# A fused cross-attention and gated feed-forward kernel on one core: steps change their place in the order of issue

## The reference

```python
def rmsnorm(x, w):
    return x * rsqrt(mean(x * x) + 1e-6) * w

# cross-attention
text = layernorm(x)                       # over the width
f    = rmsnorm(ctx, fn_w)
Q    = rmsnorm(text @ Wq.T + Wq_b, qn_w)
K    = rmsnorm(f @ Wk.T + Wk_b, kn_w)
attn = softmax(Q @ K.T / sqrt(1024))
x    = x + tanh(g_xattn) * (attn @ f)

# feed-forward with 8 gated low-rank experts
z    = layernorm(x)
base = z @ W_base.T + b_base
gate = softmax(z @ W_gate.T)
thr  = sigmoid(z @ W_thr + b_thr) * 0.125
w    = relu(gate - thr); w = w / (sum(w), or 1 where that is 0)
h    = z @ A.T                            # 8 experts x 16
moe  = sum over experts (h * w) @ B * 2
x    = x + tanh(g_ffn) * (base + moe)
```

## Time and profile before

| what | value |
|---|---|
| time, median of 3 runs | 473.6 us (472.96 to 475.18) |
| profiled execution, its span | 473.6 us |
| PE busy | 468.0 us, 99% |
| DVE busy | 361.7 us, 76% |
| ACT busy | 173.8 us, 37% |
| POOL busy | 119.8 us, 25% |
| DMA | 84.40 MB, 178 GB/s in the mean |
| key-weight stage (`m`) on PE | 85.05 to 107.27 us |
| products with `gram` (`y`, `s`, `attend`) on PE | 107.27 to 239.6 us |
| last stage, pair 0 | 239.6 to 272.4 us |
| last stage, pairs 1 to 7 | 272.4 us to the end |

### The profile page before, as it was taken

The page is one execution under the profiler, slowest core; times in us unless marked ns, Lnnn a source line. Parts: engine busy times, 40 slices in busy tenths (PEclk is TensorE's granted clock), DMA queues, the critical chain, the costliest instruction groups (busy, mean ns, idle before and its releaser), DMA issues.

```text
span 473.6 us, 6945 instructions
## 1 busy us (share of the span) xinstructions
PE 468.0 (99%) x2481; PEld 399.3 (84%) x2481; DVE 361.7 (76%) x750; ACT 173.8 (37%) x349; POOL 119.8 (25%) x107
## 2 busy tenths in 40 slices
PE   8999999999999999999999999999999999999997
PEld 7898999998887888888888888878888888888886
DVE  1687996588888978879987888968777678877733
ACT  5847532332224305226334625342241421414300
POOL 0020511002344253345242406031230502205000
PEclk9999999999999999999999999999999999999999
DMA  8993129958576378576379640221405032050202
GB/s 320 412 408 118 76 90 389 405 183 286 197 246 248 133 252 283 193 292 229 141 273 419 277 144 36 81 98 46 133 1 175 4 89 90 2 177 1 89 1 89
DMA packets 22114, 84.40 MB, mean 178 GB/s; under 512 B 2624, under 2 KB 3904, under 8 KB 19264
## 3 DMA queue, kind: packets, MB, share of 16 engines
q1 hardware_dynamic: 21792, 83.81, 48.2%
q10 hardware_dynamic: 288, 0.15, 0.1%
HBM read 61.93 MB, written 22.02 MB: 177 GB/s over the span
## 4 chain that ended last, share of the span: by engine, by line
PE 78%; DVE 8%; DMA 8%; issue 3%; ACT 1%; POOL 1%; SPq 0%; DVEq 0%; ACTq 0%
PE bank L769 10%; PE bank L773 10%; PE bank L771 10%; PE bank L649 6%; PE bank L685 5%; PE bank L687 5%; PE bank L686 5%; PE bank L530 4%; PE bank L742 4%; DMA xst<-x_dram 3%; DMA T_low<-t_low_T 2%; DMA xz<-xt_dram 2%; DMA out_dram<-xs 2%; PE bank L599 2%; DVE wl_B L1438 1%
## 5 line engine op out<-in xcount | busy, mean ns | idle before, releaser
L1554 POOL TENSOR_TENSOR small<-small,tiny 128x1 f32<-128x1 f32 (+2 forms) x25 | 23.6, 942 | 167.1 <-DVE small L1183 137.9
L1534 DVE SCALAR_TENSOR_TENSOR xs<-bank,tiny,xs 128x512 f32<-128x512 f32 (+1 forms) x61 | 43.3, 739 | 20.6 <-PE bank L773 14.9
L685 PE MATMUL bank<-xth,gram 128*128 128x512 f32 x144 | 57.3, 398 | 0.0
L687 PE MATMUL bank<-xtl,gram 128*128 128x512 f32 x144 | 56.3, 391 | 0.0
L686 PE MATMUL bank<-xth,gram 128*128 128x512 f32 x144 | 56.1, 390 | 0.0
L769 PE MATMUL bank<-wh_B,zh 128*128 128x512 f32 x116 | 47.0, 405 | 0.1
L769 PE MATMUL bank<-wh_T,zh 128*128 128x512 f32 (+1 forms) x116 | 46.6, 402 | 0.0
L1582 POOL TENSOR_TENSOR sq_sum<-sq_sum,sq 128x512 f32<-128x512 f32 x24 | 32.0, 1333 | 56.5 <-DVE sq L1362 56.5
L773 PE MATMUL bank<-wh_B,zl 128*128 128x512 f32 x116 | 45.6, 393 | 0.0
L771 PE MATMUL bank<-wl_B,zh 128*128 128x512 f32 x116 | 45.4, 391 | 0.0
L773 PE MATMUL bank<-wh_T,zl 128*128 128x512 f32 (+1 forms) x116 | 44.7, 386 | 0.0
(11 more groups left out here) (200 smaller groups left out, 1133.2 us busy)
## 6 DMA issues: line engine op xcount, KB each, us to landing
xst<-x_dram SPq DMA_DIRECT2D x16, 512.0 KB, 4.4
xz<-xt_dram SPq DMA_DIRECT2D x16, 512.0 KB, 7.6
out_dram<-xs SPq DMA_DIRECT2D x14, 512.0 KB, 2.7
xa<-x_dram SPq DMA_DIRECT2D x12, 512.0 KB, 3.4
x<-xa SPq DMA_DIRECT2D x12, 512.0 KB, 3.0
xs<-x SPq DMA_DIRECT2D x12, 512.0 KB, 4.0
wq_raw<-wq_dram SPq DMA_DIRECT2D x8, 512.0 KB, 13.8
t_raw_T<-wb_dram SPq DMA_DIRECT2D x4, 1024.0 KB, 16.7
```

The lines of the kernel that those rows point to most:

```text
L685: pe.matmul(acc[:, :], gram[:, g, 0, :], xth[b % 2][:, r, :], start=r == ROWS[j][0], stop=False)
L687: done = pe.matmul(acc[:, :], gram[:, g, 0, :], xtl[b % 2][:, r, :], start=False, stop=r == ROWS[j][-1])
L1534: dve.scalar_tensor_tensor(out=xs[slot][:, cols], in0=bank[n_bank][:, 0:hi - lo], scalar=tg[:, 1:2], in1=xs[slot][:, cols], op0=ALU.mult, ...
```

## The change

Five groups of steps change their place in the list. No instruction is added or removed, and no tile or wait changes.

1. In the key-weight stage `x_stat 6` goes from behind `m_out 1` to behind `m_out 2`, `x_stat 7` and `z 0 0` from behind `m_out 2` to behind `m_out 3`, `z 0 1` from behind `m_out 3` to behind `m_out 4`.
2. In batches 1 to 3, after `y b 2`, `shares` and `fn_low` go ahead of the next batch's `z` and `zh` quarter 0.
3. `bias 1` goes from ahead of `y 3 7` to behind it.
4. In pair 0 `split B22 1` goes from behind `mt 0` to right behind `split B22 0`, ahead of `fn_norm 3` and `chosen 1`.
5. In pairs 1 to 6 `stat t1`, the statistics of the second tile, goes from behind the second product to behind the third, and so behind `mt` of the second tile and, in pair 1, behind `split T4 0`.

```diff
--- before.py
+++ after.py
@@ -377,8 +377,8 @@
         for r in range(KB):
             first += [("m", r), ("m_out", r)]
             first += [("zh", 0, r - 3)] * (3 <= r < 7)
-            first += {0: [("x_stat", 5), ("load_xt", 0)], 1: [("x_stat", 6)], 2: [("x_stat", 7), ("z", 0, 0)],
-                      3: [("z", 0, 1)], 4: [("z", 0, 2), ("zl", 0, 0)], 5: [("z", 0, 3), ("zl", 0, 1)],
+            first += {0: [("x_stat", 5), ("load_xt", 0)], 1: [], 2: [("x_stat", 6)], 3: [("x_stat", 7), ("z", 0, 0)],
+                      4: [("z", 0, 1), ("z", 0, 2), ("zl", 0, 0)], 5: [("z", 0, 3), ("zl", 0, 1)],
                       6: [("zl", 0, 2)], 7: [("zl", 0, 3)]}[r]
         first += [("load_xt", 1)]
         for b in range(B):
@@ -389,10 +389,12 @@
                               3: [("bb",), ("bias", 0)],
                               5: [("zt", 0, "a11"), ("stat", 1)],
                               6: [("zt", 0, "a12"), ("xn", 1), ("head_w",)],
-                              7: [("zt", 0, "a21"), ("bias", 1)]}.get(j, [])
+                              7: [("zt", 0, "a21")]}.get(j, [])
                 if j == 1 and b + 1 < B:
                     first.append(("mr", b + 1))
                 first.append(("y", b, j))
+                if (b, j) == (B - 1, 7):
+                    first.append(("bias", 1))
                 if (b, j) == (B - 1, 4):
                     first.append(("load_hd",))
                 if b == 0:
@@ -400,6 +402,8 @@
                     first += {4: [("load_fn", 0)], 6: [("load_xa", 0), ("load_xa", 1)], 7: [("load_bb",)]}.get(j, [])
                 if b == 1 and 1 < j < 4:
                     first.append(("x_stat", 12 + j))
+                if b > 0 and j == 2:
+                    first += [("shares", b - 1), ("fn_low", b - 1)]
                 if b == 2 and j == 1:
                     first += [("load_xs", 0, 0), ("load_xs", 0, 1)]
                 if b == B - 1 and j == 0:
@@ -411,7 +415,7 @@
                 if j == 6 and b + 1 < B:
                     first.append(("fn_norm", b))
                 if b > 0:
-                    first += {0: [("tops", b - 1)], 1: [("norms", b - 1), ("fn_split", b - 1), ("weights", b - 1)], 2: [("shares", b - 1), ("fn_low", b - 1)],
+                    first += {0: [("tops", b - 1)], 1: [("norms", b - 1), ("fn_split", b - 1), ("weights", b - 1)],
                               3: [("load_fn", b)]}.get(j, [])
                     if j > 3:
                         t = (b - 1) * TPB + j - 4
@@ -443,7 +447,7 @@
                              7: [("zt", q, "a12"), ("sum_low", q, "s2"), ("sum_high", q, "s4")]}
                 else:
                     ahead = {0: [("attend", t0)] * attends + [("stat", t0)],
-                             1: [("attend", t1)] * attends + [("xn", t0), ("stat", t1)],
+                             1: [("attend", t1)] * attends + [("xn", t0)], 2: [("stat", t1)],
                              3: [("zt", q, "a21"), ("zt", q, "a22"), ("xn", t1), ("sum_high", q, "s1"), ("bias", t0)],
                              4: [("zt", q, "a11"), ("sum_high", q, "s3"), ("sum_high", q, "s2"), ("sum_low", q, "s1"),
                                  ("sum_low", q, "s3")],
@@ -453,9 +457,9 @@
             if p == 0:
                 last += [("hd", 0, 0), ("w_load", "T4"), ("tops", B - 1), ("gates", 0),
                          ("norms", B - 1), ("split", "B12", 1)]
-                extra = {0: [("weights", 3), ("chosen", 0), ("stat", 3), ("hd", 0, 1), ("gates", 1), ("shares", 3), ("split", "B22", 0), ("fn_norm", 3),
-                             ("chosen", 1)],
-                         1: [("mt", 0), ("split", "B22", 1)],
+                extra = {0: [("weights", 3), ("chosen", 0), ("stat", 3), ("hd", 0, 1), ("gates", 1), ("shares", 3), ("split", "B22", 0), ("split", "B22", 1),
+                             ("fn_norm", 3), ("chosen", 1)],
+                         1: [("mt", 0)],
                          2: [("pt", 3), ("load_bt",), ("fn_split", 3)], 3: [("w_load", "T3")], 4: [("fn_low", 3)],
                          5: [("mt", 1), ("bt",)]}
             else:
```

## The result

| | before | after |
|---|---|---|
| median of 18 runs each | 473.74 us (472.43 to 475.50) | 475.11 us (474.34 to 476.15) |
| ratio, 95% interval | | 1.0029 (1.0019 to 1.0039) |
| profiled execution, its span | 473.6 us | 472.8 us |

A forecast was written before the change was run, and what follows sets the result against it. PE, busy 99% of the span at full clock, was taken as the bound, with 2.2 us of stalls to win. Terms +0.88 - 0.79 + 0.38 + 1.50 - 0.40 = +1.57 us on 473.6 gave 475.2; range 472.5 to 476.5.

The forecast's parts named there:

- Edit 1, +0.88: Key-weight stage: DVE waits ahead of `m_out 4`, so `y 0 3` starts at 112.64, not 111.86, plus 0.1 restart: +0.88 us.
- Edit 2, -0.79: Batch 1: shares are made while the transfer lands, so PE's wait for `px` ahead of `pt 0` goes: -0.79 us.
- `attend 0` did not wait: Batch 1: later eviction of `pt 0` stays hidden with 0.3 us to spare; if `attend 0` waited, the term was -0.4.
- Edits 3 and 4, +0.38: `norms 3` stops waiting, but in pair 0 the low part of `mt 0` comes late and delays `zt a21`: together +0.38 us.
- the 1.1 that I forecast: Pair 0: PE idle for 1.1 us ahead of `zt a21`.
- tile 6 as what could upset the forecast: Key-weight stage: forecast wrong if tile 6 of x came some 2 us sooner or later against PE than before.
- Edit 5, +1.50 in pair 1: Pair 1: DVE's split stretches POOL's small step to 1.20 us; `zt a11` starts at 292.65, not 291.15: +1.50 us.
- Edit 5, -0.40 in pair 2: Pair 2: the second `mt`'s low part no longer stands behind waiting statistics, so `zt a22` starts 0.40 us sooner.
- every edit does what its place suggests: Whole kernel: the five stalls go and nothing becomes late, 471.2 us; chance of faster by over 0.5%: 0.10.
- The clock: Pair 1: PE's 1.5 us pause might drop the granted clock to 1.2 GHz; 4 us of that gives 477.2; chance 0.08.

The follow-up runs named there:

- first own version: Kernel before plus edits 2, 3, edit 1 keeping `z 0 1` behind `m_out 3`, edit 5 without pair 1, `fn_norm 3` behind `pt 3`: 475.52 us, ratio 1.0027.
- edit 5 with the split behind: Kernel before plus edit 5, with both halves of pair 1's T4 split behind the second tile's statistics: 475.83 us, ratio 1.0043.
- second own version: Kernel before plus edits 2, 3, edit 5 with T4 split behind statistics; pair 0: `chosen 1` before B22 splits, `fn_norm 3` behind `mt 0`: 473.13 us, ratio 0.9981.

## Why the prediction was right, and where it was not

Forecast 475.2 us from 473.6, +1.57; measured +1.37 (0.9 to 1.8). The time is right and so are the chains. But four of the five terms depend on when a transfer lands (tile 6 of x, the tokens for `z 2 0`, B22, and the tile of pair 2), and the trace of before was no typical one: its span lies 1.7 us above the median. The prediction took it for typical because "the profiled execution (473.6) equals the median", which sets a span beside a device time; the forecast itself was added to the device time and is not shifted by that. That the number came out so close is in part luck, as point 3 and the last part of this section show.

1. *Edit 1, +0.88.* The chain is exact. With edit 1, `y 0 3` starts 16.37 us after DVE begins tile 6 in the changed kernel's profile (111.55 - 95.17, and 16.38 in both others with this order); I had 112.64 - 96.27 = 16.37. In the old order it is 15.58 in the trace of before, and no profile has the stage shorter than 27.72. But DVE began tile 6 12.9 us after `m 0` in the trace of before and 11.6 to 12.8 us after it in the thirteen others. In the mean the first column has 27.95 for nine profiles in the old order and 28.45 for the three with edit 1: +0.50, and 0.14 more for the restart, which the second column shows (36.66 against 36.52). The term is +0.6 in the profiles. But tile 6 was early in those three (11.9 to 12.2 us after `m 0`); an estimate that puts 16.37 behind each of the nine landings in the old order gives +0.69, with the restart +0.8. Timed, edit 1 alone measured 1.8 (0.9 to 2.7), and leaving it out 1.0. One reading was wrong without effect: `m_out 3` is ahead of tile 7's statistics only, not of tile 6's; `z 0 0` follows tile 6 by as much as before either way.
2. *Edit 2, -0.79.* Second column: 37.30 in the mean of the seven profiles without it, 36.52 with it: -0.78. Timed 0.8. `attend 0` did not wait. The mean hides what the term is made of: `pt 0` stood for 0.07 us in one of the seven (edits 3 and 4 alone), where the transfer had landed early, and for 1.35 in another (edit 1 alone). With edit 2 there is no stall even where the transfer landed as late as in that one (the changed kernel).
3. *Edits 3 and 4, +0.38.* This term has the wrong sign in the profiles: 32.02 against 32.76, and 32.06 in the mean of the three with both edits against 32.46 in that of seven without, -0.40. The step that failed was to take the landing of B22 from the one trace. The split that waits for it starts on ACT 11.0 to 11.3 us after the start of pair 0 in the thirteen other profiles, and 12.2 us after it in that of before. At 11.0 the low part of `mt 0` is just in time for `zt a21` (254.61 + 0.28 against 254.95); at 12.2 it would be late by the 1.1 that I forecast. B22 itself landed 12.1 us after the start of pair 0 in the trace of before and 10.4 to 11.3 in the others; in ten of the thirteen the split did not wait for it at all. I had named tile 6 as what could upset the forecast, and should have named B22 with it.
4. *Edit 5, +1.50 in pair 1.* 29.39 against 27.97 in the two profiles, +1.42; the mean of the four in the new order is 29.42, that of seven in the old one 28.10 (the first own version with its late `part` left out), +1.32, as the old order is not free of stalls either (its `part` waits for the statistics and these for a tile, 0.4 us in three of seven). From the start of the first half of the split to the end of POOL's step I had 4.76, and 4.75 came (289.39 - 284.64). The step took 1.20 us in both profiles shown. The lock that the Trainium skill describes (SBUF — State Buffer, "SBUF: two separate sides") is borne out from its other side as well: the two biases of POOL held up DVE's two splits, 6.56 us for 2.4.
5. *Edit 5, -0.40 in pair 2.* 27.95 against 28.41, -0.46; in the mean of five profiles in the old order 28.30: -0.35.

Of the rivals, "every edit does what its place suggests" is out: edits 1 and 5 alone are slower beyond their intervals. The clock did not fall: it is full in all 40 slices of the page of the changed kernel, with its pause of 1.4 us in pair 1, and in those of the two profiles with one of 1.8 us (edit 5 with the split behind, second own version).

**What the profiles do not hold.** By the means above the change costs +0.64 - 0.78 - 0.40 + 1.32 - 0.35 = +0.4 us, by the estimate for edit 1 in point 1 +0.6; the runs say 1.4 (0.9 to 1.8). Span against span, eight of the twelve experiments' profiles lie within 0.2 us of the median of their kernel, two are 0.4 to 0.6 under it, the one without edit 4 is 1.4 under and the second own version 1.9 above. So the profiled executions are not faster than the timed ones as a rule. Added up over all stages, the means of the columns give 472.5 us for the old order, where the runs have 471.9 (471.8 to 472.3 beside the experiments), and 472.9 for the changed kernel, where they have 473.3. Fourteen profiles, three or four of them in a new order at any place, do not settle a difference of 1 us. In which stage the rest lies stays open. My sum came nearer to the runs than these means do, but it did so with a term of the wrong sign in the profiles, edits 3 and 4, and from a trace that was late: the chains are shown, but they alone do not account for how close the total came.

## What to carry to other kernels

A step that is moved past another is moved on every engine that has a part in it, and what it delays is found queue by queue: what stood behind it on DVE, on ACT and on POOL, and which bank or tile PE waits for next. Where a wait is to be taken away, put into its place something that does not wait for the same engine (`z 0 1` there cost nothing, `m_out 4` 1.4 us of DVE). And take a landing time from several profiles before a term rests on it: the arithmetic held within 0.1 us wherever I had followed a queue, and failed where I had not (`fn_norm 3` on POOL, the splits behind the bias), while landings moved by 1.2 to 2.1 us from one execution to the next. Before a trace is reckoned from, compare its span with the spans of the timed runs, and not with their device times: here that would have shown it to be 1.7 us late.

## What the runs showed of the hardware that I had not expected

- DVE subtractions with two SBUF inputs and POOL's additions shut each other out in either direction, and with a queue of them on each side they took turns: two splits of 1.2 us took 3.22 and 3.41 us on DVE beside two biases of 2.4 us, which took 2.40 and 3.38. The trace of before had it already (2.90 us at 289.92). Moving the splits so that POOL's work was ready earlier did not help: 1.0043 against 1.0033 for edit 5 alone.
- After a stall the second matmul of 512 columns starts 0.34 us after the first, and not 0.23 (111.55 and 111.89 in the changed kernel's profile). A like step, 0.31 us, stands without a stall where such matmuls follow a group of transposes (148.87 in the same profile).
- A load of 512 KB (tile 6 of x), issued 0.4 to 0.8 us after the start of `m 0`, landed 11.6 to 12.9 us after it from one execution to another, 11.2 to 12.3 us from its issue.
